# Attention kernel: products with values of both heads in two 64-column tiles, denominators from sums of probabilities

## What is computed

```
xn = ln(x); xt = ln(x)
spatial  = out(softmax(q k / 8) v)                  # of xn, 8 heads of 64, expert idx_s
temporal = xt + out(softmax(causal(q k / 8)) v)     # of xt, expert idx_t
fused    = out(softmax(q k / 8) v)                  # q of spatial, k and v of temporal
x = x + fused; x = x + mlp(ln(x))
```

## Time and profile before

| | us |
|---|---|
| median of 3 runs | 1923.94 |
| lowest and highest | 1919.29, 1926.11 |
| the profiled execution | 1924.25 |
| its span | 1922.5 |
| TensorE busy | 1782.2 |
| VectorE busy | 1193.4 |
| ScalarE busy | 723.1 |
| GpSimd busy | 356.6 |
| mean granted TensorE clock | 0.972 of full |

### The profile page before, as it was taken

The page is one execution under the profiler, slowest core; times in us unless marked ns, Lnnn a source line. Parts: engine busy times, 40 slices in busy tenths (PEclk is TensorE's granted clock), DMA queues, the critical chain, the costliest instruction groups (busy, mean ns, idle before and its releaser), DMA issues.

```text
span 1922.5 us, 31032 instructions
## 1 busy us (share of the span) xinstructions
PE 1782.2 (93%) x10495; PEld 1606.7 (84%) x10495; DVE 1193.4 (62%) x2345; ACT 723.1 (38%) x1346; POOL 356.6 (19%) x355
## 2 busy tenths in 40 slices
PE   2999988876999999999999999989999999899998
PEld 1788656746899999998989889889999999697996
DVE  7678678874656556654765746665656665774332
ACT  1223211034755445445455544354545544120110
POOL 3213101003213011020100003100000012564440
PEclk9999999977999999999999999999999999999999
DMA  3101000011031000030000000000000002111111
GB/s 111 34 7 45 12 12 25 9 60 39 6 124 44 28 12 7 1 124 12 12 12 12 6 1 18 23 12 12 6 12 7 6 1 76 44 60 44 44 33 54
DMA packets 24782, 58.00 MB, mean 30 GB/s; under 512 B 2537, under 2 KB 4805, under 8 KB 24013
## 3 DMA queue, kind: packets, MB, share of 16 engines
q1 hardware_dynamic: 24650, 56.18, 9.0%
HBM read 44.87 MB, written 11.30 MB: 29 GB/s over the span
## 4 chain that ended last, share of the span: by engine, by line
PE 83%; DVE 8%; issue 3%; DMA 2%; DVEq 2%; ACT 1%; POOL 1%; SPq 0%; POOLq 0%; ACTq 0%
PE ps L2320 22%; PE ps L2205 13%; PE ps L2375 7%; PE ps L2263 6%; PE ps L2302 6%; PE ps L2306 6%; PE ps L1991 5%; PE ps L2404 4%; PE ps L2128 3%; PE ps L2004 2%; PE ps L2331 1%; DMA tok_a<-in_x 1%; DVE share L1759 1%; DVE onehot L1582 1%; DVE max_part L1742 1%
## 5 line engine op out<-in xcount | busy, mean ns | idle before, releaser
L2320 PE MATMUL ps<-p_raw,v_ones 125*128 125x250 f32 x2080 | 529.1, 376 | 9.7 <-DVE feat L1761 6.2
L1742 DVE TENSOR_REDUCE max_part<-ps 125x2 f32<-125x500 f32 x520 | 330.4, 675 | 215.5 <-PE ps L2263 204.9
L1316 ACT ACTIVATE p_raw<-ps 125x500 f32<-125x500 f32 x520 | 304.4, 587 | 333.7 <-PE ps L2306 329.1
L2320 PEld LDWEIGHTS ps<-p_raw,v_ones 125*128 125x128 f32 x2080 | 362.1, 191 | 36.7 <-issue 7.7
L1759 DVE RECIPROCAL share<-ps 64x250 f32<-64x250 f32 x120 | 206.3, 1719 | 86.1 <-PE ps L2320 83.5
L2302 PE MATMUL ps<-q_both_a,k_both_a 128*125 128x250 f32 x520 | 184.2, 374 | 1.8 <-issue 1.8
L2302 PE MATMUL ps<-q_both_b,k_both_b 128*125 128x250 f32 x520 | 182.5, 372 | 0.0
L909 POOL CAST w_hi<-w_raw 128x512 fp32r<-128x512 f32 x44 | 28.3, 644 | 811.2 <-issue 353.2
L1582 DVE TENSOR_SCALAR onehot<-iota_h,win_key,key_t 125x320 f16 x453 | 177.0, 391 | 0.3 <-issue 0.3
L2205 PE MATMUL ps<-xa_hi,w_hi 128*128 128x418 f32 (+1 forms) x448 | 150.3, 335 | 13.3 <-POOL w_lo L911 9.1
L1581 DVE TENSOR_SCALAR onehot<-iota_h,low_t 125x125 f16 x453 | 128.7, 284 | 48.2 <-issue 28.1
(11 more groups left out here) (390 smaller groups left out, 3440.3 us busy)
## 6 DMA issues: line engine op xcount, KB each, us to landing
w_raw<-in_w_mlp SPq DMA_DIRECT2D x32, 256.0 KB, 2.7
w_raw<-in_w_gps SPq DMA_DIRECT2D x16, 256.0 KB, 2.6
w_raw<-in_w_tp SPq DMA_DIRECT2D x16, 256.0 KB, 2.6
w_raw<-in_w_sp SPq DMA_DIRECT2D x12, 256.0 KB, 2.6
w_raw<-in_w_cr SPq DMA_DIRECT2D x12, 256.0 KB, 2.6
d_xt<-xb_hi SPq DMA_DIRECT2D x1, 2508.0 KB, 9.3
d_xt<-xb_lo SPq DMA_DIRECT2D x1, 2508.0 KB, 14.9
xa_hi<-d_xt SPq DMA_DIRECT2D x1, 2508.0 KB, 9.9
```

The lines of the kernel that those rows point to most:

```text
L1316: act.activation(p_raw[:, g % PR, :], ps[0:TOK, g % 2, 0:4 * TOK], ACT.Exp, scale=SCALE).then_inc(s_exp, 1)
L1742: dve.tensor_reduce(part[:, y, :, j], ps[0:TOK, bank, 0:4 * TOK].rearrange("p (h k) -> p h k", h=2), AX.X, ALU.max)\
L2320: ins = pe.matmul(ps[:, bank, 0:2 * TOK], v_ones[:, n % 2, kt, h:h + 2, :], p_raw[:, g % PR, cols], start=(b == 0 and x == 0), stop=last)
```

## The change

- The steps run pass, unit, block of keys, head: both heads of a block of keys follow one another. The ring of probabilities has six slots.
- `product` is issued once for two steps, behind the side work of the second. For each of the two key tiles it has a matmul for head 0, with 64 stationary columns and output rows 0 to 63, and one for head 1, output rows 64 to 127, columns 0 to 249 of the same bank. `v_rows` holds values alone.
- The ones leave these matmuls. The probabilities are first added over a unit's blocks of keys, head 0 by GpSimd (`add_first_head`), head 1 by VectorE (`add_second_head`), 125x500 each, 200 additions on each engine, into `p_sum`. Once per unit, `denominator` ("D") multiplies 64 columns of ones with both sums, four matmuls into columns 250 to 499 of the unit's bank. It stands behind the first products of the next unit. Where a unit has a single block of keys, it takes the probabilities themselves.
- `unit_out` is done once for both heads: a reciprocal of 128x250 and a multiplication of 128x250, at the third step after the unit's last.
- Waits on semaphores follow this; the plane of pass 6 is split at another step; two constants that nothing read, with their four copies at the start, are gone.

```diff
@@ -133,7 +130,7 @@
 LEAD = 1
-PR = 3
+PR = 6
@@ -142,11 +139,15 @@
     return i + 1 if CAUSAL[n // 4] else 5
-STEP = [(n, i, h, b) for n in range(PASSES) for i in range(5) for h in range(2) for b in range(blocks_in(n, i))]
+STEP = [(n, i, b, h) for n in range(PASSES) for i in range(5) for b in range(blocks_in(n, i)) for h in range(2)]
 STEP_NO = {s: g for g, s in enumerate(STEP)}
 FIRST = {(n, i): STEP_NO[n, i, 0, 0] for n in range(PASSES) for i in range(5)}
 FIRST[PASSES, 0] = len(STEP)
-LAST = {(n, i): STEP_NO[n, i, 1, blocks_in(n, i) - 1] for n in range(PASSES) for i in range(5)}
+LAST = {(n, i): STEP_NO[n, i, blocks_in(n, i) - 1, 1] for n in range(PASSES) for i in range(5)}
+ADDED = [(n, i, b) for n in range(PASSES) for i in range(5) for b in range(1, blocks_in(n, i))]
+ADD_NO = {at: x + 1 for x, at in enumerate(ADDED)}
@@ -349,7 +350,13 @@
                 steps.append(("S", g + LEAD))
-            steps += SIDE[g] + [("P", g)]
+            steps += SIDE[g]
+            n, i, b, h = STEP[g]
+            if h == 1:
+                steps.append(("P", g))
+                if b == 0 and g - 1 > first:
+                    steps.append(("D", 5 * n + i - 1))
+        steps.append(("D", 5 * STEP[end - 1][0] + 4))
@@ -528,11 +535,12 @@
         q_row = [sb(f"q_row_{x}", [128, QR, 2 * TOK], F32R) for x in "ab"]
-        v_ones = sb("v_ones", [TOK, 2, NT, 3, 64], F32)
+        v_rows = sb("v_rows", [TOK, 2, NT, 2, 64], F32)
+        ones_f = sb("ones_f", [TOK, 64], F32)
         p_raw = sb("p_raw", [TOK, PR, 4 * TOK], F32)
+        p_sum = sb("p_sum", [TOK, 2, 4 * TOK], F32)
         xb_tmp = sb("xb_tmp", [128, 2, NODES // 2], F32)
         o_plane = sb("o_plane", [128, 2, TP], F32R, place["end"] - 4 * NODES // 64 * 64 - 64)
-        share = sb("share", [128, 2 * TOK], F32)
@@ -1024,12 +1035,25 @@
             pool.memset(max_col[:, :, :, :], 0.0).then_inc(s_clear, 1)
-            pool.memset(v_ones[:, :, :, 1, :], 1.0).then_inc(s_clear, 1)
+            pool.memset(ones_f[:, :], 1.0).then_inc(s_clear, 1)
             pool.memset(mask_turned[:, :], 0.0).then_inc(s_turned, 1)
             pool.wait_ge(s_turned, 1)
             pool.affine_select(out=mask_turned[:, :], in_=mask_turned[:, :], compare_op=ALU.is_ge, fill=NEG, base=-TOK,
                                pattern=[[1, 3 * TOK]], channel_multiplier=-1).then_inc(s_turned, 1)
+            def add_first_head(g):
+                n, i, b, _ = STEP[g]
+                pool.wait_ge(s_exp, g + 1)
+                if b == 1:
+                    pool.wait_ge(s_den, 5 * n + i)
+                if ADD_NO[n, i, b] > 1:
+                    pool.wait_ge(s_add_a, ADD_NO[n, i, b] - 1)
+                before = p_raw[:, (g - 2) % PR, :] if b == 1 else p_sum[:, 0, :]
+                pool.tensor_tensor(p_sum[:, 0, :], before, p_raw[:, g % PR, :], ALU.add).then_inc(s_add_a, 1)
             for g in range(len(STEP)):
+                if STEP[g][3] == 0 and STEP[g][2] > 0:
+                    add_first_head(g)
@@ -1312,7 +1336,12 @@
                 if g >= PR:
-                    act.wait_ge(s_pv, g - PR + 1)
+                    n, i, b, h = STEP[g - PR]
+                    act.wait_ge(s_pv, (g - PR) // 2 + 1)
+                    if blocks_in(n, i) == 1:
+                        act.wait_ge(s_den, 5 * n + i + 1)
+                    else:
+                        act.wait_ge((s_add_a, s_add_b)[h], ADD_NO[n, i, max(b, 1)])
@@ -1432,11 +1461,6 @@
             dve.tensor_copy(identb[:, :], ident[:, :]).then_inc(s_constv, 1)
-            dve.wait_ge(s_const, 4)
-            for half in range(2):
-                s, o = slice(ROW * half, ROW * half + ROW), slice(ROW * (1 - half), ROW * (1 - half) + ROW)
-                dve.tensor_copy(identb_half[s, :], ident[o, :]).then_inc(s_constv, 1)
-                dve.tensor_copy(mask_half[s, :], causal_mask[o, :]).then_inc(s_constv, 1)
@@ -1751,15 +1775,24 @@
                         .then_inc(s_max_col, 1)
-            def unit_out(g):
-                n, i, h, _ = STEP[g]
-                u, own, other = unit_of(g), HALF[h], HALF[1 - h]
-                dve.wait_ge(s_pv, g + 1)
-                dve.reciprocal(share[own, :], ps[other, 2 + u % 2, 0:2 * TOK]).then_inc(s_share, 1)
+            def add_second_head(g):
+                n, i, b, _ = STEP[g]
+                dve.wait_ge(s_exp, g + 1)
+                if b == 1:
+                    dve.wait_ge(s_den, 5 * n + i)
+                if ADD_NO[n, i, b] > 1:
+                    dve.wait_ge(s_add_b, ADD_NO[n, i, b] - 1)
+                before = p_raw[:, (g - 2) % PR, :] if b == 1 else p_sum[:, 1, :]
+                dve.tensor_tensor(p_sum[:, 1, :], before, p_raw[:, g % PR, :], ALU.add).then_inc(s_add_b, 1)
+            def unit_out(u):
+                out = feat[:, u // 5 % 4, 2 * TOK * (u % 5):2 * TOK * (u % 5 + 1)]
+                dve.wait_ge(s_den, u + 1)
+                dve.reciprocal(out, ps[:, 2 + u % 2, 2 * TOK:4 * TOK]).then_inc(s_share, 1)
                 dve.wait_ge(s_share, u + 1)
-                dve.tensor_tensor(feat[own, n % 4, 2 * TOK * i:2 * TOK * (i + 1)], ps[own, 2 + u % 2, 0:2 * TOK], share[own, :],
-                                  ALU.mult).then_inc(s_o, 1)
+                dve.tensor_tensor(out, ps[:, 2 + u % 2, 0:2 * TOK], out, ALU.mult).then_inc(s_o, 1)
@@ -1788,10 +1821,7 @@
                     fold_bias()
-            def ends(g):
-                n, i, _, b = STEP[g]
-                return b == blocks_in(n, i) - 1
+            OUT_AT = {LAST[n, i] + 3: 5 * n + i for n in range(PASSES) for i in range(5) if (n, i) not in ((7, 4), (11, 4))}
@@ -1828,11 +1858,13 @@
                             last_out(task)
+                    if STEP[g][3] == 1 and STEP[g][2] > 0:
+                        add_second_head(g)
                     for what, *at in SIDE[g]:
                         if what == "M":
                             maximum(*at)
-                    if g > first and ends(g - 1):
-                        unit_out(g - 1)
+                    if g in OUT_AT:
+                        unit_out(OUT_AT[g])
@@ -2308,17 +2342,33 @@
             def product(g):
-                n, i, h, b = STEP[g]
+                n, i, b, _ = STEP[g]
                 bank = 2 + unit_of(g) % 2
                 pe.wait_ge(s_exp, g + 1)
                 left(("P", g))
                 for z in range(3):
-                    if min(uses(n, z)) == g:
+                    if min(uses(n, z)) == g - 1:
                         pe.wait_ge(s_turn_in, 3 * n + z + 1)
                 for x in range(2):
                     kt, cols, last = 2 * b + x, slice(2 * TOK * x, 2 * TOK * (x + 1)), b == blocks_in(n, i) - 1 and x == 1
-                    ins = pe.matmul(ps[:, bank, 0:2 * TOK], v_ones[:, n % 2, kt, h:h + 2, :], p_raw[:, g % PR, cols], start=(b == 0 and x == 0), stop=last)
+                    for h, r in enumerate(HALF):
+                        ins = pe.matmul(ps[r, bank, 0:2 * TOK], v_rows[:, n % 2, kt, h, :], p_raw[:, (g - 1 + h) % PR, cols],
+                                        start=(b == 0 and x == 0), stop=last)
                 ins.then_inc(s_pv, 1)
+            def denominator(u):
+                n, i = u // 5, u % 5
+                bank, g = 2 + u % 2, FIRST[n, i]
+                if blocks_in(n, i) > 1:
+                    pe.wait_ge(s_add_a, ADD_NO[n, i, blocks_in(n, i) - 1])
+                    pe.wait_ge(s_add_b, ADD_NO[n, i, blocks_in(n, i) - 1])
+                for x in range(2):
+                    for h, r in enumerate(HALF):
+                        total = p_sum[:, h, :] if blocks_in(n, i) > 1 else p_raw[:, (g + h) % PR, :]
+                        ins = pe.matmul(ps[r, bank, 2 * TOK:4 * TOK], ones_f[:, :], total[:, 2 * TOK * x:2 * TOK * (x + 1)],
+                                        start=(x == 0), stop=(x == 1))
+                ins.then_inc(s_den, 1)
```

More of the change, by code:

```diff
@@ L159, in uses @@
     t0, nt = TB[b]
-    return [STEP_NO[n, i, h, x] for i in range(5) for h in range(2) for x in range(blocks_in(n, i)) if t0 <= 2 * x + 1 and 2 * x < t0 + nt]
+    return [STEP_NO[n, i, x, h] for i in range(5) for h in range(2) for x in range(blocks_in(n, i)) if t0 <= 2 * x + 1 and 2 * x < t0 + nt]
 def value_turns(n):
@@ L288, in pool_plan @@
     folded = AT["F", FB] + 8
-    for n, start in ((0, folded), (1, folded), (2, FIRST[3, 1]), (3, FIRST[4, 2]), (4, FIRST[7, 0] + 2), (5, FIRST[7, 0] + 2), (6, FIRST[7, 0] + 6),
+    for n, start in ((0, folded), (1, folded), (2, FIRST[3, 1]), (3, FIRST[4, 2]), (4, FIRST[7, 0] + 2), (5, FIRST[7, 0] + 2), (6, FIRST[7, 1]),
                      (8, FIRST[11, 0] + 4), (9, FIRST[11, 0] + 4), (10, FIRST[11, 2])):
@@ L359, in unit_of @@
 def unit_of(g):
-    n, i, h, _ = STEP[g]
-    return 10 * n + 2 * i + h
+    n, i, _, _ = STEP[g]
+    return 5 * n + i
 def bank_plan():
@@ L372, in bank_plan @@
             use = [entry[1] % 2]
+            slot = entry[1] - LEAD
         elif kind == "P":
```

(18 more changed lines are left out.)

17 lines of the change are left out of this document (7 added, 10 removed).

## The result

The kernel after takes 1909.02 us (median of 4 runs, 1908.73 to 1912.08) against 1922.23 for the kernel before on the same chip (4 runs, 1919.29 to 1926.11): ratio 0.9927, interval 0.9911 to 0.9943, about 14 us faster. Forecast were 1887 and 37 us. The sign was right, the size wasn't. The profiled execution of after took 1912.08 us, its span is 1910.3; the profiled spans differ by 12.2 us.

The account below looks back on a forecast made before the run. TensorE's occupied time was taken as the bound. From 1924.25 us, products -164, denominators +50, round trips +68, exponentials +7 and ends +2 gave -37: 1887 us. The range for 8 in 10 was 1805 to 1960.

Parts of the forecast that it names:

- Products: Attention products on TensorE: a pair of steps falls from 1.68 to 1.05 us, 260 times, saving 164 us.
- if passes start in order: In TensorE's queue, head 1's first pass waits behind head 0's second, so four products take five slots, 1.05 us.
- rival A: Attention products overlap fully, each array half in its own order: four slots a pair, -219 us, 1832 us; chance 0.25.
- Round trips: TensorE going to 64-column tiles and back costs 0.26 us, 260 times: 68 us added, bounds 0 and 91.
- Denominators: New products of ones on TensorE, four slots or 0.84 us for each of 60 units: 50 us added.
- Exponentials: Second product's exponential loses 0.84 us of cover; 31 of 260 have less slack than that: 7 us added.
- Cost: nothing, under that cover: VectorE's additions, net +16 us of its work, cost no time, since it already waits 205 us for the maxima's matmuls.
- rival C: Additions in VectorE's queue ahead of the maxima hold TensorE up: 72 us at half their length, 1959 us; chance 0.12.
- Ends: After the last products of the two halves, denominators precede reciprocal and multiplication with TensorE otherwise idle: 2 x 1 us.

Follow-up runs that it names:

- experiment 1: Kernel after, but both products of head 0 are issued ahead of the two of head 1 instead of alternating heads: 1917.0 us, 0.9964 of the kernel before.
- Experiment 4: Kernel after, but denominators stand alone between scores and side work instead of right behind a product: 1942.4 us, 1.0101 of the kernel before.
- Experiment 3: Kernel after, but GpSimd adds the output bias to the residual only after the last denominators: 1906.36 us, 0.9903 of the kernel before.

## Why the prediction was off

**Products: -164 us, from five slots for a pair. Wrong, by the step "if passes start in order".** The trace of after has four slots, and experiment 1 shows why: the halves keep their own orders even if the queue doesn't alternate them. The term was -219, rival A's. I had chosen between the bounds by an argument about the queue for which the trace of before had no row.

**Round trips: +68. The size was off.** 260 x 0.34 to 0.36 is 88 to 94. The nearest row, one stationary column, gave 0.26, too little; the upper end of the bound, 0.35, is what came. Its reason, the longer load of 64 columns, fits but isn't shown. Experiment 4 confirms the price with 58 more round trips. The Trainium skill, "TensorEngine Tiling (Array Packing)", Key Properties, has both sides of this: tiles that work independently, and a drain where the mode changes. By both rules, the trace agrees, and the drain's price here is in the 0.34 us.

**Denominators: +50. Right** (0.845 us each).

**Together:** for each pair, before had 437 us of products (0.84 each). After has 260 x 1.20 + 60 x 0.845 = 363, or 360 with 1.19. TensorE's work fell by 75 us or a little more, where the three terms forecast 46.

**Exponentials: +7. Right in kind and size:** 7.3 us of waits of products and 4.6 of scores, 12 against 3.5 in before. Part of that is luck. Counted again in the trace of before, 64 of the 260 second steps of a pair (85, if the second head's steps are meant) have under 0.84 us of slack, not 31, and lack 15 to 21 us together, not 6.4. And cover was asked for exponentials alone: that the product also covered the queries' way to the maxima (+9 us, line 2297) was put at nothing without being looked at.

**VectorE: "Cost: nothing, under that cover". Wrong, and this is the step that decides the case.** The load was right (64%). But the reasoning was that an addition ahead of a step's maxima can't matter since these need scores that lie behind, and that VectorE waits 205 us anyhow. Neither looks at the one place where TensorE waits for VectorE at once: the transposition, which needs the last maxima of a unit a few matmuls after they were issued. There the addition stands ahead, and the block of reciprocal and multiplication with it. This is rival C's mechanism, "additions in VectorE's queue ahead of the maxima". Its price was put at 72 us on top; shown are 21 to 28 us of the stretch, clock included (experiments 10, 7 and 2, which take the additions to another engine, behind the maxima, or away).

In the stretch the terms are: -75 for TensorE's work; +44 for longer stands (74 us against 30: transposition of the maxima +29, maxima +10, scores +5, denominators and others +5, products -5); about +6 for stands of exponentials too short for that count; +14 for the clock (27 us more at the low level, half of them lost). That is -11 against -18 measured, so 7 us aren't accounted for. Of the 29, 16 go with the additions (experiments 2 and 7).

**Ends: +2 us. Wrong:** 10 us. The last addition of VectorE is queued behind normalisations which GpSimd slows. The trace of before had the row for it, the addition of 5.09 us beside VectorE's normalisation, and I had named it as contention but not asked what stands behind it at the end. Experiment 3 gives 7 us of it back, and the other 3 are about what was forecast.

**Sum.** -18 in the stretch, +10 in the tail, -4 of scatter at the start: -12 of the span. With A's slots, round trips of 91 and ends of 2 the forecast's own sum would have been about -69, and VectorE's queue, the lost cover, the clock and the tail took the greater part of it. The kernel with the maxima first comes out at 1890 us, near the forecast's 1887, but by other terms; the agreement is chance.

## What to carry to other kernels

When an engine gets new work, ask for each of the other engines' immediate waits (matmul, reduction, matmul on its result) what now stands ahead of the reduction in its queue; the share of busy time says nothing on it, and moving one call behind another was worth 19 us here. A matmul that is moved or made shorter was also cover for the results that its neighbours wait for; measure what it hid (0.84 us at each of nine first maxima here). And where work of one engine falls away, look at the clock too: most stands of 2 to 3 us were followed by pieces at half the clock.

## What the runs showed of the hardware

- Two f32 matmuls of 64 stationary columns in the two halves of the array run together completely: starts 6 to 8 ns apart, eight passes of 250 columns in four slots of 0.21 us, whether or not the queue alternates them (block 0.996 or 1.003 us; not alternated, the two of a pair start 13 ns apart).
- Going from full width to 64 columns and back costs 0.34 to 0.36 us (after: 0.15 in the block of 0.996, 0.09 ahead of it, 0.10 behind).
- Behind a stand of TensorE of 2.6 us (after, 810.92 to 813.55) the granted clock was 0.51 for 3.4 us, though TensorE was busy all through.
- A reciprocal of 128x250 takes as long as one of 64x250 (1.713 and 1.719 us), so one of 128 rows replaces two of 64 at half the time:

```profile
L1787 DVE TENSOR_TENSOR p_sum<-p_sum,p_raw 125x500 f32<-125x500 f32 x144 | 116.4, 808 | 100.6 <-ACT p_raw L1345 98.4 <-issue 0.3
L1793 DVE RECIPROCAL feat<-ps 128x250 f32<-128x250 f32 x60 | 102.8, 1713 | 40.4 <-PE ps L2369 40.2
L1787 DVE TENSOR_TENSOR p_sum<-p_raw 125x500 f32<-125x500 f32 x56 | 54.4, 971 | 0.5
```

- VectorE's addition takes 0.67 us alone and up to 1.74 beside work of GpSimd on SBUF (1618.01, beside the bias additions); 57 of the 200 took over 0.9 us, each overlapping an instruction of GpSimd, 171 us for all, 37 more than 200 x 0.67. Another 58 overlap one and are no slower. The Trainium skill, "SBUF — State Buffer", SBUF: two separate sides, has the two engines exclude one another at a shared pair of ports; by that rule, the trace agrees, though with 37 us instead of the 258 that the prediction gave as the most.
